# Coefficient loads in permuted order, one transpose moved forward, seven weight tiles scaled on ScalarE: a fused normalise, depthwise convolution and projection kernel

## What is computed

```
v  = group_norm(x)                       # 32 groups of one channel: mean and variance per image and channel
xd = concat(v[:, :, 0::2, 0::2], v[:, :, 0::2, 1::2], v[:, :, 1::2, 0::2], v[:, :, 1::2, 1::2])   # 128 channels, 32 x 32
f  = concat(dwconv(xd, w1, 1), dwconv(xd, w3, 3), dwconv(xd, w5, 5))    # 384 channels, depthwise, zero padded
y  = einsum('bchw,oc->bohw', f, w_proj)  # w_proj: 128 x 384
out = x + y scattered back to 32 channels of 64 x 64
```

## Time and profile before

| what | value |
|---|---|
| median of 3 runs | 135.24 us (135.13 to 135.46) |
| profiled execution, its own time | 135.7 us |
| its span on the engines | 133.9 us |
| busy: PE, DVE, POOL, ACT | 124.9, 125.0, 119.9, 110.3 us |
| mean granted TensorE clock | 0.986 of full speed |

### The profile page before, as it was taken

One profiled execution on the slowest core, in us unless ns is written; L12 is line 12 of the kernel. 1 busy time (PEld: TensorE's weight loads), 2 busy tenths in 40 slices (PEclk: granted clock), 3 DMA queues, 4 the chain that ended last, 5 costly groups with the idle time before them and its releaser, 6 DMA issues.

```text
span 133.9 us, 1668 instructions
## 1 busy us (share of the span) xinstructions
PE 124.9 (93%) x514; PEld 96.8 (72%) x514; DVE 125.0 (93%) x234; ACT 110.3 (82%) x116; POOL 119.9 (90%) x92
## 2 busy tenths in 40 slices
PE   6968999999999999999999999999999999999910
PEld 6955788888886887688886888688877688578700
DVE  6679999999979999999999999999999999999960
ACT  2389979999999999999999999999999999160010
POOL 6269879999999999999999999999999999999970
PEclk9999999999999999999999999999999999999995
DMA  4999999880044008097979873989299919897876
GB/s 136 260 250 201 207 209 201 169 167 0 5 81 81 0 0 161 5 117 95 187 115 117 155 168 39 91 144 190 30 100 134 186 37 115 91 110 145 182 159 143
DMA packets 35944, 16.68 MB, mean 125 GB/s; under 512 B 34144, under 2 KB 34272, under 8 KB 35552
## 3 DMA queue, kind: packets, MB, share of 16 engines
q0 software_dynamic: 1488, 6.93, 38.8%
q1 hardware_dynamic: 32784, 9.11, 35.6%
q10 hardware_dynamic: 1664, 0.54, 1.7%
HBM read 5.46 MB, written 4.19 MB: 72 GB/s over the span
## 4 chain that ended last, share of the span: by engine, by line
POOL 62%; issue 16%; DVE 12%; PE 4%; POOLq 1%; ACT 1%; ACTq 0%
POOL RING_SUM L343 56%; DVE ACC L649 4%; POOL X L393 3%; PE YP L691 3%; POOL LO L330 2%; DVE st L546 2%; DVE weff L600 2%; DVE whi L608 1%; POOLq L102 1%; DVE ACC L645 1%; DVE stp L552 1%; DVE HI L623 1%; PE YP L795 1%; POOL rstd L312 0%; POOL wlo L385 0%
## 5 line engine op out<-in xcount | busy, mean ns | idle before, releaser
L343 POOL TENSOR_TENSOR RING_SUM<-RING_SUM,PROD 128x900 f32<-128x900 f32 (+1 forms) x45 | 93.0, 2072 | 3.4
L649 DVE SCALAR_TENSOR_TENSOR ACC<-G,coef,ACC 128x480 f32<-128x480 f32 (+3 forms) x132 | 82.4, 742 | 0.0
L476 ACT ACTIVATE PROD<-G,coef 128x900 f32<-128x900 f32 (+1 forms) x45 | 44.5, 1051 | 0.0
L723 PE MATMUL YP<-HI,wlo 128*128 128x512 f32 (+1 forms) x146 | 38.1, 412 | 0.0
L723 PE MATMUL YP<-HI,whi 128*128 128x512 f32 (+1 forms) x146 | 36.2, 398 | 1.7 <-DVE HI L623 1.2
L723 PE MATMUL YP<-LO,whi 128*128 128x512 f32 (+1 forms) x146 | 36.0, 398 | 0.0
L723 PEld LDWEIGHTS YP<-HI,wlo 128*128 128x128 f32 x146 | 27.5, 189 | 8.6 <-issue 2.9
L723 PEld LDWEIGHTS YP<-HI,whi 128*128 128x128 f32 x146 | 27.2, 189 | 8.7 <-DVE HI L623 1.3
L723 PEld LDWEIGHTS YP<-LO,whi 128*128 128x128 f32 x146 | 27.5, 189 | 6.7 <-issue 0.5
L438 ACT ACTIVATE G<-X,nbias,rstd 64x1024 f32<-64x1024 f32 x16 | 21.1, 1321 | 1.2 <-DVE nbias L564 0.9
L459 ACT ACTIVATE Y<-YP 64x1024 f32<-64x1024 f32 x14 | 15.4, 1097 | 3.4 <-PE YP L778 3.1
(11 more groups left out here) (69 smaller groups left out, 66.4 us busy)
## 6 DMA issues: line engine op xcount, KB each, us to landing
LO<-G POOLq DMA_DIRECT2D x7, 527.5 KB, 5.3
X<-in_x_dram SPq DMA_DIRECT2D x14, 256.0 KB, 5.5
X<-Y POOLq DMA_DIRECT2D x6, 512.0 KB, 7.3
out_dram<-X SPq DMA_DIRECT2D x12, 256.0 KB, 4.5
XS<-in_x_dram SPq DMA_DIRECT2D x1, 512.0 KB, 6.1
out_dram<-X SPq DMA_DIRECT2D x4, 128.0 KB, 2.2
X<-in_x_dram SPq DMA_DIRECT2D x2, 136.0 KB, 4.4
XS<-in_x_dram SPq DMA_DIRECT2D x1, 256.0 KB, 3.3
```

The lines of the kernel that those rows point to most:

```text
L343: pool.tensor_tensor(dst, dst, prod(b, k), ALU.add).then_inc(prod_added, 1)
L476: act.activation(prod(b, k), g_tap(b, POOL_OF[b][k + 1]), ACT.Copy, scale=of5(POOL_OF[b][k + 1])).then_inc(prod_ready, 1)
L649: dve.scalar_tensor_tensor(half_part(ACC, tap, h), half_tap(b, tap, h), of5(tap), half_part(ACC, tap, h), ALU.mult, ALU.add).then_inc(acc_ ...
L723: mm = nc.tensor.matmul(dst, w[:, n, :], src, start=start, stop=False, skip_group_check=True)
```

## The change

The coefficients of w5, w3 and w1 are no longer loaded into `w_sb` and permuted by a matmul. Each is loaded straight into `coef` by two DMAs, one for each half j of the 64 partitions, whose source walks the channels in the order i, c. Those of w5 and w3 are issued by ACT, those of w1 by SP, between the bottom part of image 0 and `XS` of image 1. The two coefficient matmuls, the two ACT copies, `w_sb` and the semaphores coef_ready and coef_copied go. The third part of wp is transposed ahead of `sum_parts(0)`, into another PSUM bank, and has its own count on wt_ready. ACT scales seven tiles instead of five, six of them ahead of `high_half`, POOL two instead of four, one of them ahead of `inv_std`. On DVE the first three `add_w3` stand ahead of `part_bias`. WARM becomes (19, 6).

```
-WARM = (20, 5)
+WARM = (19, 6)
-ACT_SCALED = 5
+ACT_SCALED = 7
+        def load_coef(eng, w, c0, c1, s):
+            src = w.rearrange("(i j c) a h w -> j i c (a h w)", i=2, j=2)
+            for j in range(2):
+                eng.dma_start(coef[HALF * j:HALF * (j + 1), c0:c1], src[j]).then_inc(s, 16)
...
@@ SP, behind load_image(sp, 0, image_loaded[0], TOP, PH) @@
+            load_coef(sp, w1, W1_AT, N_COEF, w1_loaded)
@@ POOL @@
-            inv_std(1, 0, 1)
             pool.wait_ge(wpT_ready, 1)
-            pool.wait_ge(coef_copied, 1)
+            pool.wait_ge(w5_loaded, 32)
             scale_w5(ACT_SCALED)
+            inv_std(1, 0, 1)
@@ ACT @@
-            act.dma_start(w_sb[:, 0:W3_AT], w5.rearrange("c a h w -> c (a h w)")).then_inc(w_loaded, 16)
-            act.dma_start(w_sb[:, W3_AT:W1_AT], w3.rearrange("c a h w -> c (a h w)")).then_inc(w_loaded, 16)
-            act.dma_start(w_sb[:, W1_AT:N_COEF], w1.rearrange("c a h w -> c (a h w)")).then_inc(w1_loaded, 16)
+            load_coef(act, w5, 0, W3_AT, w5_loaded)
+            load_coef(act, w3, W3_AT, W1_AT, w3_loaded)
 ...
-            act.activation(wpT[:, :], WT_PS[:, 2 * P:3 * P], ACT.Copy).then_inc(wpT_ready, 1)
-            act.wait_ge(coef_ready, 1)
-            act.activation(coef[:, 0:W1_AT], COEF_PS[:, 0:W1_AT], ACT.Copy).then_inc(coef_copied, 1)
+            act.activation(wpT[:, :], SMALL[:, 0:P], ACT.Copy).then_inc(wpT_ready, 1)
 ...
-            scale_w5(0, CHUNK)
+            scale_w5(0, ACT_SCALED - 1)
 ...
-            scale_w5(CHUNK, ACT_SCALED)
-            act.wait_ge(coef_ready, 2)
-            act.activation(coef[:, W1_AT:N_COEF], COEF_PS[:, W1_AT:N_COEF], ACT.Copy).then_inc(coef_copied, 1)
+            scale_w5(ACT_SCALED - 1, ACT_SCALED)
@@ DVE @@
-            dve.wait_ge(wt_ready, 1)
-            dve.wait_ge(coef_copied, 1)
+            dve.wait_ge(wt_ready, 2)
+            dve.wait_ge(w3_loaded, 32)
+            add_w3(0, 1, 2)
             part_bias(0)
-            add_w3(0, 1, 2)
@@ PE @@
+            pe.wait_ge(ident_permuted, 1)
+            transpose(2, SMALL[:, 0:P]).then_inc(wt_ready, 1)
             sum_parts(0)
-            pe.wait_ge(ident_permuted, 1)
-            for n, k in enumerate((2, 1, 0)):
-                ...
-            mm.then_inc(wt_ready, 1)
-            pe.wait_ge(w_loaded, 32)
-            coefficients(0, W1_AT)
+            transpose(1, WT_PS[:, P:2 * P])
+            transpose(0, WT_PS[:, 0:P]).then_inc(wt_ready, 1)
 ...
-            pe.wait_ge(w1_loaded, 16)
-            pe.wait_ge(coef_copied, 1)
-            coefficients(W1_AT, N_COEF)
```

More of the change, by code:

```diff
@@ L122, in build @@
         wp_sb = sb("wp_sb", [P, 3 * P], F32)
-        w_sb = sb("w_sb", [P, N_COEF], F32)
         coef = sb("coef", [P, N_COEF], F32)
@@ L152, in build @@
         WT_PS, SMALL = YP[:, 2, 0:512], YP[:, 2, 512:1024]
-        COEF_PS = SMALL[:, 200:200 + N_COEF]
         SPREAD_PS = [YP[:, 1, 512 * n:512 * n + PARTS * STATS] for n in range(2)]
@@ L160, in build @@
         xs_loaded = [sem(f"xs_loaded{n}") for n in range(3)]
-        wp_loaded, w_loaded, w1_loaded = sem("wp_loaded"), sem("w_loaded"), sem("w1_loaded")
-        coef_ready, coef_copied = sem("coef_ready"), sem("coef_copied")
+        wp_loaded, w5_loaded, w3_loaded, w1_loaded = sem("wp_loaded"), sem("w5_loaded"), sem("w3_loaded"), sem("w1_loaded")
         stat_const, part_stats, spread_done = sem("stat_const"), sem("part_stats"), sem("spread_done")
@@ L358, in scale_w5 @@
                 pool.tensor_scalar(weff[:, n, :], wpT[:, :], of5(INNER[n]), None, ALU.mult).then_inc(pool_scaled, 1)
+            pool.wait_ge(wpT_ready, 1)
+            pool.wait_ge(w5_loaded, 32)
+            scale_w5(ACT_SCALED)
             inv_std(1, 0, 1)
-            pool.wait_ge(wpT_ready, 1)
-            pool.wait_ge(coef_copied, 1)
-            scale_w5(ACT_SCALED)
             pool.wait_ge(weff_step, CHUNK)
@@ L411, in _ @@
             act.wait_ge(wt_ready, 1)
-            act.activation(wpT[:, :], WT_PS[:, 2 * P:3 * P], ACT.Copy).then_inc(wpT_ready, 1)
-            act.wait_ge(coef_ready, 1)
-            act.activation(coef[:, 0:W1_AT], COEF_PS[:, 0:W1_AT], ACT.Copy).then_inc(coef_copied, 1)
+            act.activation(wpT[:, :], SMALL[:, 0:P], ACT.Copy).then_inc(wpT_ready, 1)
             act.wait_ge(wpT_ready, 1)
-            act.wait_ge(coef_copied, 1)
+            act.wait_ge(w5_loaded, 32)
             def scale_w5(n0, n1):
@@ L629, in _ @@
             dve.wait_ge(weff_step, N_INNER)
-            dve.wait_ge(coef_copied, 2)
+            dve.wait_ge(w1_loaded, 32)
             dve.scalar_tensor_tensor(weff[:, N_INNER - 1, :], transposed(0), coef[:, W1_AT:W1_AT + 1],
@@ L695, in _, with transpose @@
                 keep_warm(WARM_COLS)
-            def coefficients(c0, c1):
-                nc.tensor.matmul(COEF_PS[:, c0:c1], ident_ph[:, :], w_sb[:, c0:c1],
-                                 start=True, stop=True).then_inc(coef_ready, 1)
+            def transpose(k, dst):
+                pe.wait_ge(permuted, 3 - k)
+                return nc.tensor.transpose(dst, wp_ph[:, k, :], ident_ph[:, :])
             def sum_parts(b):
@@ L789, in last_ring @@
                                      start=False, stop=True, skip_group_check=True).then_inc(last_quarter, 1)
+            pe.wait_ge(ident_permuted, 1)
+            transpose(2, SMALL[:, 0:P]).then_inc(wt_ready, 1)
             sum_parts(0)
-            pe.wait_ge(ident_permuted, 1)
-            for n, k in enumerate((2, 1, 0)):
-                pe.wait_ge(permuted, n + 1)
-                mm = nc.tensor.transpose(WT_PS[:, k * P:(k + 1) * P], wp_ph[:, k, :], ident_ph[:, :])
-            mm.then_inc(wt_ready, 1)
-            pe.wait_ge(w_loaded, 32)
-            coefficients(0, W1_AT)
+            transpose(1, WT_PS[:, P:2 * P])
+            transpose(0, WT_PS[:, 0:P]).then_inc(wt_ready, 1)
             pe.wait_ge(low_zero, 2)
```

## The result

The changed kernel took 137.55 us (median of 4 runs, 136.83 to 137.79) against 135.35 before: 1.0151 times as long, with a 95% interval of 1.0105 to 1.0198. It is slower, by 2.0 us (the ratio) to 2.2 us (the medians), where 0.5 less was forecast; the time lies outside the range. Medians are over all runs, while ratios leave out the runs in a slower state that some executions of any kernel fall into, so the two can differ a little.

The account below looks back on a forecast made before the run. DVE, PE and POOL were taken as full to the end, so only an earlier start could help. T = 7.3 gave streams 0.42 to 0.68 us earlier; 0.5 off the 135.24 median made 134.75, range 134.25 to 135.6.

Parts of the forecast that it names:

- the third need of T: DVE's first w3 step needs w3 loaded; landing forecast at 7.03 to 7.33 us, the fourth issue at 2.63.
- T: Time at which DVE starts the first w3 step: 7.97 us before, forecast 7.3, bounds 6.9 to 8.2.
- The upper bound of 8.2: Latest w3 landing: four loads on two DMA engines, their packets taking turns with the image's.
- The rule against the change: A DMA is split by its slowest dimension, so two-block sources use two engines; T would be 7.4 to 8.2.
- rival 3: At DVE's first w3 step, the w3 load becomes the bound: a loss of 0.2 to 0.5 us, 135.6; chance 0.18.
- the sum for DVE and ACT: Start on DVE and ACT: `HI` at T + 1.22, first ring step at T + 6.66 to T + 6.92.
- one for one from T = 7.98: Price in rival 3: from that T on, each later microsecond of the w3 load delays the start equally.
- For PE the sum: PE's first `wlo` matmul at T + 7.36, up to 0.2 less if the wait for the second cast is shorter.
- The term put at nothing: PE's gap before image 0 would be shorter, so its granted clock would cost nothing.
- The cover of the image loads: SP's two added loads delay later ones by 0.98 us; image 5's second load stays covered at `bn` by 0.56.
- The casts: DVE's two casts took 0.49 and 1.13 us; the second might take 0.49, saving 0.64, or the first become slow.
- The gain that was forecast: An earlier start of the DVE and PE streams, 0.5 us kept to the end.

Follow-up runs that it names:

- e9: The changed kernel with SP's loads of image 0 and everything behind them held until w5 and w3 have landed; 137.03 and 139.68 us, only two runs.
- e1: The changed kernel with each coefficient load's source in one block of 64 channels, permutation left out; 135.10 us, 0.9963 of the kernel before.
- e2: The changed kernel with ten more warm matmuls, WARM = (19, 16); 136.43 us, 1.0039 of the kernel before.
- e5: The changed kernel with each load's source in four blocks of 16 channels, permutation left out; 136.30 us, 1.0038 of the kernel before.
- e10: The changed kernel with four one-block DMAs of 32 rows per coefficient load, permutation kept; 135.97 us, 1.0020 of the kernel before.
- e3: The changed kernel with the three loads, coefficient matmul and two copies of the kernel before; 135.72 us, 0.9978 of the kernel before.
- e8: The changed order with the old loads and coefficient matmul, plus four more warm matmuls, WARM = (19, 10); 135.53 us, 0.9966 of the kernel before.
- e12: e8 once more with more rounds; 135.72 us against 136.07 for the kernel before, 0.9970.
- e11: The kernel before with four more warm matmuls, WARM = (20, 9); 135.59 us, 0.9953 of the kernel before.
- e6: The changed kernel with image 0's bias ahead of the w3 steps again; 137.50 us, 1.0110 of the kernel before.
- e7: The kernel before without its five later warm matmuls, WARM = (20, 0); 136.04 us, 1.0031 of the kernel before.
- e4: The kernel before with only the loads changed to the new two-block form; 137.91 us, 1.0120 of the kernel before.

## Why the prediction was wrong

**The step that failed** is the third need of T, "the load of w3". I took 7.3, next to the rows of the small loads, and had 8.2 as the upper bound; it was 8.74. Both parts were too small. The fourth issue came at 3.38, not 2.63: the first load in two blocks took 1.08 to issue and the other three 0.51 to 0.52. And the landing came 5.3 behind it, not 4.7. The upper bound of 8.2 was worked out with the right number of engines but with packets at 0.013 to 0.026 us each from the landing of the first load on; e9 and the packets of 4.6 to 5.4 us show that they stood, for 0.8 us, while image packets ran.

**The rule against the change** was in the text, with its page, and I weighed it as if the small loads of before spoke against it. They could not: they were in one block. Those rows could bear no evidence for a form of load that they did not show, and rival 3 deserved more than 0.18.

**From T on, the sum for DVE and ACT held.** `HI` at T + 1.03 (1.22 forecast; the bias starts 0.79 behind T, where I counted 0.97 for the three steps), the first ring step at T + 6.61 (6.66 to 6.92), in e1 at T + 6.57. Rival 3's line "one for one from T = 7.98" gives 0.76 for T = 8.74, and the ring step came 0.71 later. For PE the sum was too long: where the clock stayed up, the first `wlo` matmul came at T + 6.89 (e1, e2 and e5 alike), against T + 7.16 to T + 7.36.

**The term put at nothing** is the clock. I wrote that the new gap of PE is shorter and costs nothing. It would have been longer even at the T of the forecast: PE's work ahead of image 0 ended at 8.58 before and ends at 7.81 now (7.68 in e1), and its first matmul on image 0 comes at T + 2.04 (here and in e1), so T = 7.3 makes a gap of 1.5 to 1.7 us, an estimate from these rows. With T = 8.74 it was 2.96 instead of 1.25, and the first `wlo` matmul came at T + 8.39. e2 puts this at 1.1 to 1.5 us, about as much as the late landing itself. Rival 3 was priced without it: its loss of 0.2 to 0.5 us for T = 8.2 fits e10 (T = 8.22 with the clock up, ratio 1.0020, some 0.3 us), and even with T = 8.88 e2 loses only 0.5 us by its ratio while the clock stays up. A late start of one engine has a second price where that engine's clock can fall while it waits.

**The cover of the image loads** held, though not by the sum: the two loads of w1 took SP 1.70 us, not 0.98, and `XS` of image 1 was issued at 5.59, 1.88 later than before, but by the second load of image 5 only 0.53 was left of that (17.50 for 16.97). No DMA is waited for at `bn`, neither in the changed kernel nor in e1, where that `bn` comes at 24.15, as early as the forecast wanted it. **The casts**: both short, 0.44 and 0.36. The first, beside a `wlo` of POOL that ended at 11.76, ended 0.22 behind it; the slow one of the earlier trace rows ended at 13.52, and the `wlo` it stood beside ended 0.22 earlier, at 13.30. That agrees with the rule of "SBUF — State Buffer" in the Trainium skill, "Who interferes with whom", by which a cast in the two-port mode that comes second waits until the GpSimd instruction is over. That both were short in the changed kernel is the timing of its later start, and not something that the change was built for.

**The gain that was forecast** is borne out by e1 alone: with T = 7.59 its ratio is 0.9963, with an interval that just reaches 1, and seven of its ten runs (134.86 to 135.12) are faster than the fastest of the 31 runs of the kernel before beside it (135.29). e1 leaves the permutation out, so it is no replacement. With the permutation kept and the old loads (e3, e8, e12) a gain of the new order is not shown, and the safest gain on record is e11's, four warm matmuls in the old kernel.

## What to carry to other kernels

Look at the outermost dimension of both sides of a small DMA before counting its bytes: here a source in two blocks used two of 16 engines, and beside the image loads it landed 1.2 us later than the same bytes in one block; the packets of a queue, less the rows, show how many engines a load used. Where a small load becomes a direct wait of three engines, price it from loads of its own form, or call it unknown. And when a start gets later, ask what the idle engine's clock does: the gap can cost as much again as the delay. The mean granted clock of every run, on record with its time, points to it without another profile.

## What the runs showed of the hardware

- Without image traffic, the two-block loads of w3, issued up to 3.39, had landed by 5.54; beside it they landed at 8.4 to 9.7. What orders the packets of two queues on an engine so that one stands for 0.8 us was not found out.
- Four engines (e5) helped w5 by 0.6 us and w3 not at all.
- A gap of PE does not decide alone whether the clock falls: it stayed at 1.00 behind gaps of 1.95 (e1), 2.18 (e6) and 2.38 us (e5) and fell behind 1.44 (e3), 1.77 (e9), 1.89 (e7), 2.96 (the changed kernel) and 4.24 us (e4), in one profiled run each. Over ten runs each, the same kernel can do both (e5, e6, the kernel before).
